# Local attention between a mixer and two transformer layers: scores on 64 contraction rows, even and odd heads on the two row halves of the array

## What is computed

```python
qkv = shift_token(x) @ wqkv                 # 128 -> 3 * 512, 8 heads of 64
q, k = l2norm(q) * qs, l2norm(k) * ksc
q, k = rotary_xpos(q, k)
# windows of 64 tokens; the keys are those of the window and of the one before it
sim = einsum('bhwid,bhwjd->bhwij', q * 8, keys)
sim = where((i < j) | (i > j + 64) | (j == -1), -max, sim)
o = einsum('bhwij,bhwjd->bhwid', softmax(sim), values)
x = x + o @ wo
# then shift_token, layer norm, 128 -> 2 * 341, a * gelu(g), 341 -> 128, residual
```

## Time and profile before

| what | value |
|---|---|
| median of three runs | 510.57 us (510.19 to 510.65) |
| span of the profiled execution | 509.7 us |
| median above that span | 0.87 us |
| PE matmul busy | 400.0 us (78%) |
| PE weight load busy | 325.1 us (64%) |
| DVE busy | 421.6 us (83%) |
| ACT busy | 306.6 us (60%) |
| POOL busy | 191.7 us (38%) |
| mean granted clock of PE | 0.912 |

### The profile page before, as it was taken

One profiled execution on the slowest core, in us unless ns is written; L12 is line 12 of the kernel. 1 busy time (PEld: TensorE's weight loads), 2 busy tenths in 40 slices (PEclk: granted clock), 3 DMA queues, 4 the chain that ended last, 5 costly groups with the idle time before them and its releaser, 6 DMA issues.

```text
span 509.7 us, 11479 instructions
## 1 busy us (share of the span) xinstructions
PE 400.0 (78%) x3768; PEld 325.1 (64%) x3768; DVE 421.6 (83%) x1071; ACT 306.6 (60%) x884; POOL 191.7 (38%) x159
## 2 busy tenths in 40 slices
PE   2641068999998999899989998999897889787552
PEld 1330046777776877687768776877686678576432
DVE  6788968999999799969996999799778997874544
ACT  2363067686767766676768576777575677465120
POOL 2016735454645254515441454244423542330000
PEclk9795577999999999899989999999897999799856
DMA  8400241211421042105111411141114210120100
GB/s 281 132 0 0 62 105 42 73 27 31 111 61 28 18 124 50 26 18 128 47 29 35 123 36 28 48 120 28 28 27 114 51 26 15 31 49 1 22 21 21
DMA packets 42401, 28.22 MB, mean 55 GB/s; under 512 B 21700, under 2 KB 36598, under 8 KB 42358
## 3 DMA queue, kind: packets, MB, share of 16 engines
q1 hardware_dynamic: 42357, 27.68, 20.8%
HBM read 13.51 MB, written 3.15 MB: 33 GB/s over the span
## 4 chain that ended last, share of the span: by engine, by line
PE 50%; DVE 31%; issue 12%; ACT 4%; POOL 1%; DMA 1%; DVEq 1%; POOLq 0%; ACTq 0%
PE upper L624 10%; PE bank L513 5%; PE upper L602 4%; PE bank L517 4%; PE bank L514 4%; PE upper L608 4%; DVE h L1029 4%; PE bank L673 4%; PE bank L638 4%; PE upper L619 3%; DVE ss L1010 3%; DVE rn L856 2%; ACT probs L788 2%; DVE rot_sin L1004 2%; DVE neg_max L1051 2%
## 5 line engine op out<-in xcount | busy, mean ns | idle before, releaser
L788 ACT ACTIVATE probs<-upper,neg_max 128x128 f32<-128x128 f32 x256 | 90.4, 368 | 77.0 <-DVE neg_max L1051 75.1
L477 POOL TENSOR_TENSOR rot<-rot_cos,rot_sin 128x512 f32<-128x512 f32 x32 | 40.8, 1274 | 149.4 <-PE upper L573 143.0
L486 POOL TENSOR_TENSOR rot<-rot,rn 128x1024 f32<-128x1024 f32 x32 | 63.3, 1978 | 73.5 <-DVE rn L881 71.5
L513 PE MATMUL bank<-wqkv_hi,act_t_hi 128*128 128x512 f32 x96 | 43.1, 449 | 16.5 <-DVE o_tok L1061 8.5
L624 PE MATMUL upper<-k_t,q_even 128*64 128x128 f32 x512 | 56.0, 299 | 0.0
L788 ACT ACTIVATION_READ_ACCUMULATOR probs<-upper,neg_max 128x1 f32 x256 | 52.9, 206 | 0.0
L624 PE MATMUL upper<-k_t,q_odd 128*64 128x128 f32 x512 | 52.5, 286 | 0.0
L1051 DVE TENSOR_REDUCE neg_max<-upper 128x4 f32<-128x512 f32 x64 | 43.1, 682 | 4.4 <-PE upper L624 3.5
L1004 DVE TENSOR_TENSOR rot_cos<-bank,tab 128x512 f32<-128x512 f32 x64 | 43.6, 681 | 2.2 <-PE bank L517 2.2
L1010 DVE TENSOR_REDUCE ss<-sq 128x16 f32<-128x1024 f32 x32 | 38.8, 1212 | 5.7 <-ACT sq L809 5.5
L1004 DVE TENSOR_TENSOR rot_sin<-bank,tab 128x512 f32<-128x512 f32 x64 | 43.5, 679 | 0.0
(11 more groups left out here) (128 smaller groups left out, 1004.5 us busy)
## 6 DMA issues: line engine op xcount, KB each, us to landing
v_mid<-v_tok SPq DMA_DIRECT2D x64, 128.0 KB, 2.3
tab_raw<-tables SPq DMA_DIRECT2D x8, 512.0 KB, 3.5
h_tok<-group_in SPq DMA_DIRECT2D x14, 128.0 KB, 3.5
x_res<-group_in SPq DMA_DIRECT2D x28, 64.0 KB, 1.8
wqkv_raw<-wqkv SPq DMA_DIRECT2D x2, 768.0 KB, 6.5
x_in<-x SPq DMA_DIRECT2D x4, 256.0 KB, 3.7
head_scale<-head_scales SPq DMA_DIRECT2D x8, 128.0 KB, 3.7
group_in<-normed SPq DMA_DIRECT2D x4, 256.0 KB
```

The lines of the kernel that those rows point to most:

```text
L486: pool.tensor_tensor(rot[:, :, :], rot[:, :, :], rn[:, 0:2 * HEADS].unsqueeze(2).broadcast_to([P, 2 * HEADS, DH]), ALU.mult).then_inc(rot_ ...
L513: pe.matmul(out_ap, lhs, rhs, start=True, stop=False)
L788: last = act.activation(probs[:, h, :], s_bank[half][:, (h % 4) * P:(h % 4 + 1) * P], ACT.Exp, bias=neg_max[a.par][:, h:h + 1], accum_out= ...
```

## The change

Scores contract 64 rows. Bank 0 takes the even heads, from partitions 0 to 63 of q and k, bank 1 the odd heads, from partitions 64 to 127. Each of the four quarters of the array (row half times column half) gets its own small mask matmul and one small matmul for each pair of heads. q is copied once. The mask of a sequence's first tile is used for the lower window alone. Since a bank no longer holds four neighbouring heads, `mix_values` and `divide_o` pick the columns by the new order. Both increments of `s_done` come at the end, and PE has a semaphore step of its own ahead of the masks (`settle`).

```diff
-    first = band & ((r >= WINDOW) | (c >= WINDOW))
+    first = band & (c >= WINDOW)
...
-        q_even = sb("q_even", [P, PAIRS, P])
-        q_odd = sb("q_odd", [P, PAIRS, P])
+        q_t = sb("q_t", [P, PAIRS, P])
...
-            pool.memset(q_even[:, :, :], 0.0).then_inc(init_done, 1)
-            pool.memset(q_odd[:, :, :], 0.0).then_inc(init_done, 1)
...
-            def scores(a, half):
-
-
-                if half == 0 and a.slot == 0:
+            def scores(a):
+
+                if a.slot == 0:
                     pe.wait_ge(k_carried, a.group + 1)
-                need(pe, (pt_saved0, pt_saved1)[half], a.t)
-                b = s_bank[half]
-                pe.matmul(b[:, :], ident_bf[:, :], mask_bf[1 if a.first else 0][:, :], start=True, stop=True)
-                for h in range(4 * half, 4 * half + 4):
-                    q, col = (q_even, q_odd)[h % 2][:, h // 2, :], (h % 4) * P
-                    keys = k_t[:, h // 2, a.slot * P:]
+                need(pe, pt_saved0, a.t)
+                need(pe, pt_saved1, a.t)
+                settle(pe)
+                for low in (0, 64):
+                    for half in range(2):
+                        rows = slice(64 * half, 64 * half + 64)
+                        pe.matmul(s_bank[half][low:low + 64, :], ident_bf[rows, rows],
+                                  mask_bf[1 if a.first and low == 0 else 0][rows, :], start=True, stop=True)
+                for p in range(PAIRS):
                     for low in (0, 64):
-                        last = pe.matmul(b[low:low + 64, col:col + P], q[:, low:low + 64], keys[:, low:low + P],
-                                         start=False, stop=True, skip_group_check=True)
-                last.then_inc(s_done, 1)
+                        for half in range(2):
+                            rows = slice(64 * half, 64 * half + 64)
+                            at = a.slot * P + low
+                            last = pe.matmul(s_bank[half][low:low + 64, p * P:(p + 1) * P], q_t[rows, p, low:low + 64],
+                                             k_t[rows, p, at:at + P], start=False, stop=True, skip_group_check=True)
+                            if p == PAIRS - 1 and low == 64:
+                                last.then_inc(s_done, 1)
...
                 for h in range(HEADS):
-                    cols = slice(h * DH, (h + 1) * DH)
+                    head = 2 * (h % PAIRS) + h // PAIRS
+                    cols = slice(head * DH, (head + 1) * DH)
...
-                        pe.wait_ge(q_saved, 2 * (prev.t + 1))
+                        pe.wait_ge(q_saved, prev.t + 1)
...
-                        scores(prev, 0)
-                        scores(prev, 1)
+                        scores(prev)
...
-                        act.copy(q_even[0:64, :, :], qt_bank[0:64, :].rearrange("p (c t) -> p c t", c=PAIRS)).then_inc(q_saved, 1)
-                        act.copy(q_odd[64:128, :, :], qt_bank[64:128, :].rearrange("p (c t) -> p c t", c=PAIRS)).then_inc(q_saved, 1)
+                        act.copy(q_t[:, :, :], qt_bank[:, :].rearrange("p (c t) -> p c t", c=PAIRS)).then_inc(q_saved, 1)
...
-                dve.tensor_tensor(o_tok[:, :].rearrange("p (h d) -> p h d", h=HEADS),
-                                  o_bank[:, :].rearrange("p (h d) -> p h d", h=HEADS),
-                                  inv_sum[:, :].unsqueeze(2).broadcast_to([P, HEADS, DH]), ALU.mult).then_inc(o_ready, 1)
+                split = lambda ap: ap.rearrange("p (c f d) -> p f c d", f=2, d=DH)
+                inverse = inv_sum[:, :].rearrange("p (f c) -> p f c", f=2).unsqueeze(3).broadcast_to([P, 2, PAIRS, DH])
+                dve.tensor_tensor(split(o_tok[:, :]), split(o_bank[:, :]), inverse, ALU.mult).then_inc(o_ready, 1)
```

More of the change, by code:

```diff
@@ L214, in sandwich_kernel @@
         dve_chain = sem("dve_chain")
-        settled = {e.name: sem(f"settled_{e.name}") for e in (mybir.EngineType.SP, mybir.EngineType.DVE, mybir.EngineType.Pool)}
+        settled = {e.name: sem(f"settled_{e.name}") for e in (mybir.EngineType.SP, mybir.EngineType.DVE, mybir.EngineType.Pool, mybir.EngineType.PE)}
         block = ctx.enter_context(nc.Block())
@@ L676, in feed_forward @@
                 last.then_inc(down_done, 1)
-            pe.wait_ge(init_done, 5)
+            pe.wait_ge(init_done, 3)
             pe.wait_ge(const_bf, 3)
```

## The result

The changed kernel takes 517.4 us (median of 19 runs, 511.9 to 523.8), the kernel before 511.15 in as many runs beside it (509.8 to 514.0). The ratio is 1.008, 95% interval 1.0056 to 1.0103: **slower**, by under 1% but clear of the noise, where 505.7 and a range of 502 to 512.5 had been forecast. That ratio is taken over the twelve shorter runs of the nineteen, whose median is 515.3 us; the other seven took 520.3 us and more. The runs go with PE's granted clock: the run of 511.9 us has a mean of 0.912, the one of 523.8 us 0.881. The profiled execution took 520.9 us, with a span of 519.1.

What follows compares the result with a forecast made beforehand. It took a circle of POOL's sums, DVE's work, exponentials and transposes as the bound, without scores. Terms 3.9 + 1.7 + 1.7 - 2.4 took 4.9 us off 509.7; span 504.8 plus 0.87 gave 505.7 us, range 502 to 512.5.

Steps and rivals of the forecast that it cites:

- New clock falls: PE's new wait before V in step 0, new in four passes: two more falls on the path, 2.4 us back.
- The likeliest case: The forecast itself, 505.7 us, with two new falls at V's waits in step 0; chance 0.67.
- The slower rival: Falls at 16 new waits before V, 1.2 us each; slower from seven on, 522 us with all; chance 0.16.
- Scores of 1.3 us: Masks and score matmuls on PE take 1.3 us a tile in place of 2.69.
- The circle of POOL, DVE, exponentials and transposes: Loop of POOL's sums, DVE's Newton steps and row maximum, exponentials and transposes bounds the kernel; scores stand outside it.
- h2_lo is late next: Step 2: the feed-forward's third matmul then waits for DVE's h2_lo, limiting the saving to 1.2 us with a fall, 0.1 without.
- PE's idle time before V: Saved PE time turns into waiting before V's projection: about 2.3 us in step 0, 1.6 in steps 1 and 2.
- The start: The first tile's scores, on the path and at half clock, and the single q copy save 1.7 us net.
- the 3.9 us: Step 2 saving over six passes: three with a clock fall at 1.2 us, three without at 0.1.
- the walk's 503.3: Forecast time if no new clock falls come, with the old ones kept.
- Small edits: Inverse pattern, PE's semaphore step, common release of both row maxima, memsets of q: all taken to cost nothing.
- no overlap: Row halves of the score matmuls run one after the other, scores stay at 2.7 us: about 509.4 us; chance 0.12.

Runs made afterwards that it cites:

- e1: Changed kernel with the Q and K products done twice in steps 0 and 2, in front of V's wait: 507.4 us, 0.991 of the kernel before.
- e6: Changed kernel with Q and K products, scores and mix_values repeated in front of waits, and e10's feed-forward order: 501.1 us, 0.986 of the kernel before.
- e10: Changed kernel with the feed-forward's four products that don't need h2_lo put ahead of the wait for it: 509.4 us, 0.994 of the kernel before.
- e4: Kernel before with both score banks released at the end of the second half: 523.6 us, 1.0245 of the kernel before.
- e3: Changed kernel with all score matmuls of one row half before the other, each bank released when done: 521.8 us, 1.019 of the kernel before.
- e8: Kernel of e3 with mix_values done twice in step 2, in front of the wait for h2: 507.8 us, 0.994 of the kernel before.
- e9: Changed kernel with mix_values done twice in step 2, in front of the wait for h2: 516.6 us, 1.010 of the kernel before.
- e5: Kernel before with half of the score matmuls left out, scores still whole-row: 504.7 us, 0.989 of the kernel before.
- e2: Changed kernel with masks and scores done twice in steps 3, 0 and 1: 510.1 us, 0.9986 of the kernel before.
- e11: Changed kernel run again without edits, beside e9 and e10, source of the second trace: 515.5 us, 1.0065 of the kernel before.

## Why the prediction was wrong

**The sum and the direction were wrong; the step that failed is "New clock falls".** It took two more falls at 1.2 us, 2.4 us back. Both terms of it were mis-sized. The count: five stretches of half clock between 84 and 480 us became eleven in the first trace and nine in the second, so six and four more on balance instead of two. The likeliest case had counted the V waits of step 0 alone, and for these two was right: in either trace two falls stand behind them up to 380 us. But behind three of these four falls the next wait is 1.9 to 2.0 us, where it is 1.5 to 1.6 without a fall and where 1.6 had been forecast, and then a fall stands behind it too, in step 1 and mostly in step 2 as well: at 142.7 and 155.9 us in the first trace, at 192.2, 205.3 and 342.1 in the second. That one fall brings on the next is read from this order; no run tests it alone. And the price: with a short fall behind one V wait the stretch from one wait for h2 to the next is 50.3 us (264.21 to 314.55), with a long one behind h2 50.9 (213.28 to 264.21), against 48.9 (314.55 to 363.47) and 49.2 (164.09 to 213.28) without any: 1.2 to 1.4 for the one and 1.7 to 2.0 for the other. That a fall behind the old wait for h2 can last twice as long was not in the prediction; I had even reckoned with fewer of the old ones at the low end. It happened three times in the first trace and not in the second, and what decides it stays open.

**The slower rival was right in its mechanism**: falls at V's waits. Its point of decision was seven new falls at 1.2 us; the first trace has six more than before, and three of its falls behind h2 are of the long sort, which carries it past that point. The second trace has four more and a span 1.1 us longer, where by the rival's prices it should still be shorter than before by some 2.5; so the gains were smaller than 7.3, or the falls dearer than 1.2, and which of the two is not shown. The rival had been given 0.16. The rate that the rows gave, three falls in five waits of 2 us, held up: of the waits of 1.85 us and more before a projection (without the two of 5 us), 5 of 9 are followed by a fall in the first trace and 5 of 10 in the second, and of those of 1.5 to 1.7 us none. What the prediction lacked was that waits of 1.6 us grow to that length once a fall stands ahead of them. The range ended at 512.5, short of the rival's own numbers.

**What was right.** Scores of 1.3 us: 1.21 to 1.28. The overlap of the row halves, for which no row stood: shown. The first and the last of the 32 score records start 0.77 us apart, where 0.93 had been taken. The estimate of 1.14 from the Trainium skill's 3.07x (TensorE: Matmul & The Clock Gate, Part 3, Measured speedup vs the span model) lies farther off. It isn't worked out in the prediction either: 0.93 at 77% of full overlap would be 1.21. The pattern of one dimension more in `divide_o` cost nothing: 691 ns a tile before and after. The circle of POOL, DVE, exponentials and transposes, in which the scores don't stand: the row maximum still starts behind `split_inputs`. **h2_lo is late next**:

```profile
267.80 0.50 PE L514 MATMUL bank<-h_lo,w_hi 128*128 128x512 f32 x1 [1.09 <-DVE h_lo L1069]
```

PE's idle time before V: 2.3 and 1.6 us forecast, 1.9 to 2.3 and 1.5 to 1.6 measured in the passes without a fall just before. The pass without a fall: 48.9 and 49.2 us, against 49.1 and 49.5, so a gain of 0.2 to 0.3 a pass stands too. The start: the first wait for h2 ends at 160.12 us in the second trace, where no fall lies before it, and at 161.50 before, so start and first pass together gained 1.4 us where some 2 had been counted. And a short fall behind h2 costs less than before, as the 3.9 us had it: in e1 the stretch that begins with one is 49.2 us (210.72 to 259.87), where it was 50.6 and 50.4. What was off, beside the falls: PE's busy time fell by 27 us and not by some 40. That e6, hardly ever at half clock in the loops, takes 501.1 us is near the walk's 503.3 without new falls, but no test of it: e6 has e10's order too, and the 503.3 still had the old falls in it.

**"Small edits".** That a common release costs nothing as long as scores take under 2 us held; e4 shows what it costs at 2.7 us, 12 us. The rival "no overlap", priced at 509.4 with both halves released at their end, took this too lightly, for e4's release is just that. It took the clock too lightly as well: with the row halves in turn, each bank released by itself, the time is 521.8 (e3), and 507.8 with the gap before h2 filled (e8).

## What to carry to other kernels

Shortening PE's work where PE then waits is not free: price the new idle time by what the clock did behind waits of that length in the trace, and count every place, before any gain is booked. A change that is right in its steps can be saved by work that nobody needs: repeats of ready products in front of the long waits turned +0.8% into -0.9% here (e1), and with the feed-forward's four products moved forward as well into -1.4% (e6). Where ready work exists that is needed, as those four products, put that into the gap first: alone it gave 6 us (e10). And take more than one trace before counting falls: two traces of one program had them at different places, and an experiment planned from one of them (e9) filled a gap that hardly mattered.

## What the runs showed of the hardware

PE's granted clock fell to half behind about every second wait of 1.85 to 2.4 us before a projection (5 of 9 and 5 of 10 in the two traces of the changed kernel, between 90 and 460 us, in different places), and behind none of the 17 waits of 1.5 to 1.7 us there. PE's busy time over the whole stretch does not tell its clock. With PE busy 324.8 us of 376 the clock was 0.94 (e3), with 311.6 us 0.98 (e5), with 304.5 and 305.7 us 0.95 and 0.93 in the two traces of the changed kernel.

Behind waits for h2 of 1.9 to 2.1 us a fall lasted either 3.4 or 6.8 us. The long sort came only where 64-row scores followed (three times in the first trace after, four times in e3), but with such scores the short sort came too (five times in e1, e2, e10 and e11). Whether the form of the scores or the place of the fall in the pass decides is not shown.

Ready work repeated in front of the waits kept the clock up: 51 us at half clock between 84 and 460 us in the changed kernel's first trace, 23 in e1, 14 in e2, none in e6.

Four quarters of the array run matmuls at once: 16 float32 matmuls of 64x64 by 128 columns take 0.97 us to the start of the next product, where the same scores by column halves took 2 x 1.04. Four whole-array matmuls of 128 columns take 0.88 us in the kernel before (L602 at 245.86, the next at 246.74), so the quarters come near four for the time of one.
